# An adaLN network of two layers: the recurrent tail, attention's weights and attention as one block, with two stages re-ordered

## The reference, cut to what matters

```python
def _L0_ffn_ref(x, ...):                       # 16 steps, one for each batch of 512 tokens
    def step(c, xt):
        ft = jax.nn.sigmoid(xt @ wf.T + c @ uf.T + bf)
        it = jax.nn.sigmoid(xt @ wi.T + c @ ui.T + bi)
        gt = jnp.tanh(xt @ wc.T + c @ uc.T + bc)
        return ft * c + it * gt, None
    c_final, _ = lax.scan(step, c0, x)
    return jnp.tanh(jnp.einsum('tbi,oi->tbo', x, wo) + c_final @ uo.T + bo)

def _L1_attn_ref(x, w_qkv, w_out, head_scales, head_dirs):
    ...
    scores = jnp.where(causal, jnp.einsum('bhqd,bhkd->bhqk', q, k) * SCALE, -jnp.inf)
    scores = scores + head_scales * (q_proj[..., :, None] * k_proj[..., None, :])
    attn = jax.nn.softmax(scores, axis=-1)
    return (attn @ v, heads side by side) @ w_out

h = _layernorm(x) * (1 + ca) + sa;  x = x + ga * mixer(h)
h = _layernorm(x) * (1 + cb) + sb;  x = x + gb * _L0_ffn_ref(h)
mod = (silu(L1_c) @ L1_wmod)                   # shifts, scales and gates of layer 1
h = _layernorm(x) * (1 + ca) + sa;  x = x + ga * _L1_attn_ref(h)
h = _layernorm(x) * (1 + cb) + sb;  x = x + gb * experts(h)
```

## Time and profile before

| what | us |
| --- | --- |
| median of 3 runs | 2698.3 (2697.41 to 2700.79) |
| the profiled execution, its own time | 2689.7 |
| its span | 2687.9 |
| PE, DVE, ACT, POOL busy | 2297.5, 1619.2, 1319.7, 483.9 |
| mixer | 0 to 672 |
| recurrent part | 687 to 1036 |
| tail, `attention_weights`, attention's prologue | 1036 to 1083.6, to 1099.5, to 1162.2 |
| attention's batches | 1162.2 to 2171, some 63 each |
| router and experts | to 2688 |

### The profile page before, as it was taken

One profiled execution on the slowest core, in us unless ns is written; L12 is line 12 of the kernel. 1 busy time (PEld: TensorE's weight loads), 2 busy tenths in 40 slices (PEclk: granted clock), 3 DMA queues, 4 the chain that ended last, 5 costly groups with the idle time before them and its releaser, 6 DMA issues. The chain is left out here.

```text
span 2687.9 us, 45298 instructions
## 1 busy us (share of the span) xinstructions
PE 2297.5 (85%) x15010; PEld 1685.1 (63%) x15010; DVE 1619.2 (60%) x3537; ACT 1319.7 (49%) x2260; POOL 483.9 (18%) x397
## 2 busy tenths in 40 slices
PE   7999999999699997378888888888888875169997
PEld 6666666666588886245555555555555565158996
DVE  4667766765454443456666666666666655766664
ACT  3555565555455556235555555555555543034442
POOL 0011011100011116100000011111000022036664
PEclk8999999999799997679999999999999987579998
DMA  4200000000100000222322232233322228245542
GB/s 112 87 0 0 0 0 0 0 0 0 32 0 0 0 0 24 67 70 74 78 73 72 71 80 72 72 75 78 81 73 71 49 87 279 52 127 124 127 93 32
DMA packets 122975, 156.64 MB, mean 58 GB/s; under 512 B 26896, under 2 KB 104096, under 8 KB 122784
## 3 DMA queue, kind: packets, MB, share of 16 engines
q1 hardware_dynamic: 108576, 130.38, 17.7%
q0 software_dynamic: 14336, 25.44, 4.8%
HBM read 96.26 MB, written 58.98 MB: 58 GB/s over the span
## 5 line engine op out<-in xcount | busy, mean ns | idle before, releaser
L1483 DVE TENSOR_REDUCE at_top<-psum 128x1 f32<-128x512 f32 (+3 forms) x1024 | 446.7, 483 | 302.4 <-PE psum L1259 301.8
L1610 ACT ACTIVATE at_probs<-psum 128x512 f32<-128x512 f32 (+1 forms) x768 | 365.8, 530 | 347.8 <-PE psum L1277 345.5
L1257 PE MATMUL psum<-at_k_stack,at_q_stack 96*128 96x512 bf16 (+3 forms) x1024 | 296.1, 316 | 127.4 <-DMA at_k_stack<-qk_parts 71.9
L1275 PE MATMUL psum<-at_q_stack,at_k_stack 98*128 98x512 bf16 (+3 forms) x1024 | 289.9, 310 | 23.5 <-ACT at_probs L1610 16.8
L1257 PEld LDWEIGHTS psum<-at_k_stack,at_q_stack 96*128 96x128 bf16 x1024 | 103.3, 101 | 228.4 <-DVE at_top L1483 101.7
L1259 PE MATMUL psum<-at_mask_q,at_ident_b 128*128 128x128 bf16 x1024 | 206.9, 228 | 0.0
L1277 PE MATMUL psum<-at_mask_k,at_ident_b 128*128 128x128 bf16 x1024 | 202.9, 224 | 0.0
L1275 PEld LDWEIGHTS psum<-at_q_stack,at_k_stack 98*128 98x128 bf16 x1024 | 102.8, 100 | 116.3 <-issue 44.7
L1293 PE MATMUL psum<-at_probs,at_values 128*32 128x512 f32 (+3 forms) x2048 | 151.1, 436 | 0.9 <-ACT at_probs L1610 0.9
L2334 POOL DMA_INDIRECT out<-ex_result,slot_tokens x64 | 119.6, 1869 | 103.8 <-DVE ex_result L2466 89.2
L2512 ACT ACTIVATE ex_mid<-psum,ex_b_up 128x512 f32<-128x512 f32 x96 | 66.2, 690 | 106.2 <-PE psum L61 104.1
(11 more groups left out here) (401 smaller groups left out, 5896.5 us busy)
## 6 DMA issues: line engine op xcount, KB each, us to landing
qk_parts<-at_q_parts SPq DMA_DIRECT2D x96, 128.0 KB
qk_parts<-at_k_parts SPq DMA_DIRECT2D x96, 128.0 KB
at_q_stack<-qk_parts SPq DMA_DIRECT2D x64, 192.0 KB
at_k_stack<-qk_parts SPq DMA_DIRECT2D x64, 192.0 KB
x_residual<-in_x SPq DMA_DIRECT2D x16, 512.0 KB, 3.8
at_q_stack<-qk_parts SPq DMA_DIRECT2D x64, 128.0 KB
at_k_stack<-qk_parts SPq DMA_DIRECT2D x64, 128.0 KB
token_rows<-ro_h_tok SPq DMA_DIRECT2D x16, 512.0 KB, 3.0
```

Of the source, the lines that this page charges most:

```text
L1257: pe.matmul(out, q_stack[0:STACK, h, qt * P:(qt + 1) * P], k_stack[0:STACK, h, 0:w], start=True, stop=True)
L1275: pe.matmul(bank(bk)[:, col:col + w], k_stack[0:STACK + N_SHIFT, h, kt * P:(kt + 1) * P], q_stack[0:STACK + N_SHIFT, h, kt * P:T], start=T ...
L1483: dve.tensor_reduce(top[:, h, qt:qt + 1], bank(MAX0 + n % 2)[:, col:col + w], AX.X, ALU.max).then_inc(mxr.sem, 1)
L1610: act.activation(probs[:, slot(h), 512 * f:512 * f + w], bank(f)[:, 0:w], ACT.Exp).then_inc(ex.sem, 1)
```

## The change

`out_x` and `out_c` now live until the end of attention. The three blocks of tail, `attention_weights` and attention become one. A tail's sum, tanh and gate are all written in place in `out_x` (the sum of batch 0 on DVE, the others on POOL). Attention's buffers are pieces of the same memory: `q_stack` that of batches 0 to 3, `k_stack` 4 to 7, `probs` and `oT` 8 to 14, `o_tok` 15; the staging of the weights lies in `values`, `v_tok` and `xn`. So the first load of a stack waits until eight tails are turned (`turned`), and the first scores until all 16 are added. Each engine's tails are written between the steps of the prologue.

The modulation of layer 1 moves into the last batch of the mixer. In the mixer, DVE does all four subtractions, ahead of `dve_hT_lo`. In the batches of attention, ACT issues the rows of maxima (`act_row`), SP only stores and loads, and the side work of ACT and DVE is placed behind single pieces f of a head, the q and k copies one head later; load 1 waits until the row of group 2 of the batch under way has landed.

```diff
-        recurrent_stage(nc, t, ps, mem)
-        attention_stage(nc, t, ps, mem)
+        with ExitStack() as seam:
+            out_x = seam.enter_context(nc.sbuf_tensor("out_x", [P, NB, DK, T], F32))
+            out_c = seam.enter_context(nc.sbuf_tensor("out_c", [P, DK, T], F32))
+            recurrent_stage(nc, t, ps, mem, out_x, out_c)
+            attention_stage(nc, t, ps, mem, out_x, out_c)
...
+            else:
+                pe.wait_ge(*gs(i, 4))
+                pe.wait_ge(wmod1_in, 16)
+                for j in range(12):
+                    for k in range(DK):
+                        last = pe.matmul(bank(MOD1_BANK)[:, j * NB:(j + 1) * NB], wmod1[:, k, j * P:(j + 1) * P],
+                                         mem["silu_c1"][:, k, :], start=(k == 0), stop=(k == DK - 1))
+                last.then_inc(mod1_done, 1)
...
+            dve.wait_ge(*ms(i, 1))
+            for m in range(IK):
+                dve.tensor_tensor(dev[:, m, :], y[:, m, :], mean[:, :], ALU.subtract).then_inc(fc0.sem, 1)
             if not last_batch:
                 dve_hT_lo(dve, i + 1, False)
-            dve.wait_ge(*ms(i, 1))
-            for m in range(2, IK):
-                dve.tensor_tensor(dev[:, m, :], y[:, m, :], mean[:, :], ALU.subtract).then_inc(fc0.sem, 1)
...
-            for m in range(2):
-                if m == 0:
-                    pool.wait_ge(*ms(i, 1))
-                pool.tensor_tensor(dev[:, m, :], y[:, m, :], mean[:, :], ALU.subtract).then_inc(dv.sem, 1)
...
-            for m, ready, n in ((2, fc0, 1), (0, dv, 1), (3, fc0, 2), (1, dv, 2)):
-                act.wait_ge(*ready(i, n))
+            for m in range(IK):
+                act.wait_ge(*fc0(i, m + 1))
                 act.activation(dev[:, m, :], dev[:, m, :], ACT.Square).then_inc(sq.sem, 1)
...
+        flat = out_x[:, :, :, :].rearrange("p s k t -> p (s k t)")
+        ROW_X = DK * T
+        q_stack, k_stack = (flat[:, 4 * n * ROW_X:4 * (n + 1) * ROW_X].bitcast(BF16).rearrange("p (h t) -> p h t", h=HEADS)
+                            for n in range(2))
+        at_probs, at_oT, at_o_tok = 8 * ROW_X, 8 * ROW_X + (GROUP + 1) * 1280, 15 * ROW_X
+        probs = flat[:, at_probs:at_oT].rearrange("p (s n) -> p s n", s=GROUP + 1)
+        oT = flat[:, at_oT:at_oT + T]
+        o_tok = flat[:, at_o_tok:at_o_tok + TT * D].rearrange("p (n d) -> p n d", n=TT)
...
+        delta = out_c
+        f_q, f_k, f_v, f_o = (values[:, n, :, :].rearrange("p h c -> p (h c)").rearrange("p (k n) -> p k n", k=DK)
+                              for n in range(4))
+        f_qT, form = (v_tok[:, 2 * n:2 * n + 2, :] for n in range(2))
+        dirs, sdirs, scales = xn[0:HEADS, 0, :], xn[0:HEADS, 1, :], xn[0:HEADS, 2, 0:1]
...
+        def pe_tail(pe, b):
+            pe.wait_ge(gated, b + 1)
+            if tail_before(b) >= 0:
+                pe.wait_ge(added, tail_before(b) + 1)
+            for n in range(TT):
+                for f in range(DK):
+                    last = pe.transpose(bank(tail_bank(b) + n // 2)[:, (n % 2) * D + f * P:(n % 2) * D + (f + 1) * P],
+                                        out_x[:, b, f, n * P:(n + 1) * P], ident[:, :])
+            last.then_inc(turned, 1)
...
+            pe_tail(pe, 0)
...
+            pe_tail(pe, 6)
+            pe_tail(pe, 7)
+            pe.wait_ge(w_const, 3)
+            pe_tail(pe, HALF_X)
+            pe.wait_ge(added, HALF_X)
...
             for h in range(AHEAD):
                 for f in range(3):
                     pe_max(pe, 0, h, f)
-            pe_turn_max(pe, 0, 0)
+                if h == GROUP:
+                    pe_turn_max(pe, 0, 0)
+                pe_tail(pe, HALF_X + 1 + h)
+            pe.wait_ge(added, NB)
+            pe.wait_ge(w_lo, O_W + 1)
...
+        def dve_tail_add(dve, b):
+            dve.wait_ge(turned, b + 1)
+            tiles = x[:, b * TT:(b + 1) * TT, :]
+            k = tail_bank(b)
+            dve.tensor_tensor(tiles, tiles, ps[:, k:k + 2, :].rearrange("p k (a d) -> p (k a) d", a=2), ALU.add
+                              ).then_inc(added, 1)
...
+            dve_tail_add(dve, 6)
+            dve_tail_add(dve, 7)
+            dve_w_lo(dve, O_W)
             dve.memset(k_stack[STACK:STACK + N_SHIFT, :, :], 1.0).then_inc(const.sem, 1)
+            dve.wait_ge(w_lo, len(WEIGHTS))
             dve.memset(values[:, :, :, HD:HD + 1], 1.0).then_inc(const.sem, 1)
             dve.memset(values[:, :, :, HD + 1:], 0.0).then_inc(const.sem, 1)
-            dve_hT_lo(dve, 1)
+            dve_tail_add(dve, HALF_X)
             for h in range(AHEAD):
                 dve_max(dve, 0, h)
-            dve_neg_max(dve, 0, 0, True)
+                if h == GROUP:
+                    dve_neg_max(dve, 0, 0, True)
...
+        def act_row(act, b, g):
+            act.wait_ge(*neg(b, N_SHIFT * (g + 1)))
+            for j in range(N_SHIFT):
+                act.dma_start(q_stack[STACK + j:STACK + j + 1, GROUP * g:GROUP * (g + 1), :].rearrange(
+                    "a h (q p) -> a (h q) p", p=P), neg_top[:, j, :]).then_inc(row[g].sem, 16)
...
+        def act_tail(act, b):
+            if b == 0:
+                act.wait_ge(z_dve, 1)
+            else:
+                act.wait_ge(z_pool, b)
+            act.activation(out_x[:, b, :, :], out_x[:, b, :, :], ACT.Tanh).then_inc(tanh_done, 1)
+            act.wait_ge(tanh_done, b + 1)
+            for m in range(DK):
+                last = act.activation(out_x[:, b, m, :], out_x[:, b, m, :], ACT.Copy, scale=mod0[:, GATE_B + m, b:b + 1])
...
+                for f in range(3):
+                    act_exp(act, i, h, f, first)
+                    if f == 2 and h % GROUP == 0 and not (first and h == 0):
+                        act_keep_oT(act, *((i, h // GROUP - 1) if h else (i - 1, NG - 1)))
+                    if h == 1 and not last:
+                        if f < 2:
+                            act_qk(act, i + 1, f)
+                        else:
+                            act_qk2(act, i + 1, 0)
+                    if f == 0 and h % GROUP == 2 and not (last and h + GROUP > HEADS):
+                        g = h // GROUP
+                        act_row(act, *((i, g + 1) if g + 1 < NG else (i + 1, 0)))
+                    if h == 2 and f < 2 and not last:
+                        if f == 0:
+                            act_qk2(act, i + 1, 1)
+                        act_qk(act, i + 1, 2 + f)
+                    if h == 3 and f < 2 and not last:
...
+            act_tail(act, 0)
+            act_tail(act, 1)
+            act_tail(act, 2)
+            act.wait_ge(w_fold, 5)
+            act_w_hi(act, Q_W)
+            act_tail(act, 3)
...
+            act_tail(act, 6)
+            act_tail(act, 7)
+            act_w_hi(act, O_W)
+            for b in range(HALF_X, NB - 1):
+                act_tail(act, b)
+            act_row(act, 0, 0)
+            act_tail(act, NB - 1)
...
+        def pool_tail_sum(pool, b):
+            pool.tensor_tensor(out_x[:, b, :, :], out_x[:, b, :, :], out_c[:, :, :], ALU.add).then_inc(z_pool, 1)
...
+            for b in range(1, 4):
+                pool_tail_sum(pool, b)
             pool_rstd(pool, 0)
+            for b in range(4, 7):
+                pool_tail_sum(pool, b)
+            pool_qk3(pool, 0, (0, 1))
             pool_rstd(pool, 1)
-            pool_qk3(pool, 0)
+            pool_qk3(pool, 0, (2, 3))
+            for b in range(7, NB):
+                pool_tail_sum(pool, b)
             pool_values(pool, 0)
...
+                if isinstance(b, int) and b == 0:
+                    sp.wait_ge(turned, HALF_X)
+            elif g == 1:
+                sp.wait_ge(*(loaded[0](0, loaded[0].per) if isinstance(b, int) and b == 0 else row[2](b - 1, row[2].per)))
...
-        def sp_row(sp, b, g):
-            sp.wait_ge(*neg(b, N_SHIFT * (g + 1)))
-            for j in range(N_SHIFT):
-                sp.dma_start(q_stack[STACK + j:STACK + j + 1, GROUP * g:GROUP * (g + 1), :].rearrange(
-                    "a h (q p) -> a (h q) p", p=P), neg_top[:, j, :]).then_inc(row[g].sem, 16)
...
+            for side in range(2):
+                sp_store(sp, i + 1, side)
+            for g in range(NG):
+                sp_load(sp, i + 1, g)
```

497 lines of the change are left out of this document (213 added, 284 removed).

## The result

The changed kernel takes 2681.6 us (median of 4 runs, 2679.5 to 2686.0), the one before 2697.9 on the same chip: ratio 0.9945, interval 0.9929 to 0.9961. It is faster by 16 us, 0.55%. The forecast was 2621 with a range of 2555 to 2668, so the sign was right, but the time is 60 us above the forecast and 14 above the range.

The account below looks back on a forecast made before the run. PE was taken to bound mixer and attention, gains coming only from its gaps, and hand-over chains the seam. -12 - 26 - 39 = -77 on 2689.7 gives 2612.7; with 8.6 carried from profile to median, 2621 us, range 2555 to 2668.

Parts of the forecast that it names:

- Mixer, -12: Mixer: with all four subtractions on DVE ahead of the low half, PE's variance wait goes; -12 us, bounds -8 to -13.
- Seam, -26: Recurrence's end to first scores: three blocks become one, first Exp at about 1136, before 1162; -26 us, bounds -40 to -10.
- (a): Seam: the chain from first weight DMA to batch 1's transposed input on ACT takes 41.9 us, now starting at 1036.
- (b): Seam: ACT does tails 3 to 7 within that chain, 12.3 us plus 3 for hand-overs; tail 7 turned at about 1095.
- Rival E: Seam: POOL's sums block DVE's two-input operations, some ten losing 1 to 2.4 us each; +20, 2641 us; chance 0.07.
- Attention batches, -39: Attention loop: earlier loads, less clock loss and shorter waits for maxima give -2.6 us a batch, times 15; bounds -90 to +15.
- Step (1): Attention batches: rows of maxima go from SP to ACT, so the load isn't held behind them; 0.3 to 0.4 us a group.
- Step (2): Attention batches: q and k copies one head later, between single Exps and reductions; the load goes out 1 us earlier.
- ACT's issues: Attention batches: each row DMA issue on ACT takes 0.58 us, mostly hidden; 0.3 to 0.4 us a group on the path.
- B: Attention loop gains nothing, as the load still comes late and ACT's row issues eat the splitting's gain; 2660 us; chance 0.20.
- the loss that eats the 38 us: Attention loop: a loss that just eats the 38 us of mixer and seam; chance 0.03.
- C: Attention loop: ACT stands at the row's wait with Exps behind it, 4.7 us a batch; slower, 2730 us; chance 0.09.

Follow-up runs that it names:

- mixer_only: The kernel before with the mixer's re-ordering alone (four subtractions on DVE, ahead of the low half): 2681.6 against 2693.3 us, ratio 0.9953.
- mix_c_sums: qk_early with group 2's row issued one piece earlier on ACT, other rows on POOL, and POOL's tail sums moved later in the seam: 2587.7 us, ratio 0.9627.
- qk_early: The changed kernel with the q and k copies back at their old places behind heads 0 and 1, in two lumps: 2616.2 us, ratio 0.9704.
- qk_late: The changed kernel with its old attention batches put back, except that the q and k copies stay one head later: 2659.1 us, ratio 0.9864.
- rows_sp: The changed kernel with only the rows of maxima back on SP in the old order: 2661.6 us, ratio 0.9910.
- loop_rows_act: The changed kernel with its attention batches as before, except that ACT issues the rows of maxima: 2637.8 us, ratio 0.9788.

## Why the prediction was wrong, point by point

**Bounds and stages.** Right: each stage moved by its own wait, and the sum over the span tells nothing.

**Mixer, -12.** Right by mechanism and size where it stands alone (mixer_only). In the changed kernel 10 us of it are left. PE's first matmul of the recurrent part stands at 691.6 us before, at 679.9 in mixer_only and at 681.6 in the changed kernel (680.9 to 682.1 in eight kernels built on it). Most of the 1.7 us between comes up in the mixer's last batch, into which layer 1's modulation was moved: its matmuls hold PE from 648.1 to 654.6 us, at a place where PE waits 4.6 us in mixer_only, and the batch is 1.8 us longer. The prediction put this term at nothing, "if the cover fails: some 2 us, once": the cover failed.

**Seam, -26.** Right in its sum, 27.3, and less so in its terms. Tail 7 was turned at about 1088 and not 1095 in a trace that is 10 us ahead, so (a) and (b) were 3 us longer than reckoned. The load took 11.5 us from issue to first maxima (1088.48 to 1100.0) for 12.5, and its wait was 8.8 of PE's. The seven heads took 3.1 to 4.1 us each, 25 in all with the scores' start, for 27. **Rival E's mechanism was there** although the total was not its: next to POOL's sums the four norms of each of two batches took 7.4 and 6.3 us and not 1.4, two low halves 5.0 and not 1.3. The rule of the Trainium skill that the prediction named ("SBUF — State Buffer", section "SBUF: two separate sides") agrees with the low halves, which have two inputs in SBUF. The norms have one large input, and what the prediction took from the rule, operations with two SBUF inputs, did not name them. That same rule of the Trainium skill also names VectorE operations in a two-port mode; whether the norms ran in one no run here shows. mix_c_sums puts the price of these rows on the seam's end at 8.6 us, so that the sum came out right in spite of them is partly luck: other terms must have been too long by about as much.

**Attention batches, -39.** Wrong; measured +29.4, or +2.0 us a batch (65.9 for 63.9; the prediction's 63.3 for before was 0.6 low) where -2.6 was forecast. Three steps failed.

- *The order on SP.* Step (1) of this part read the earlier trace rows as a load that is held up behind the row, and asked only when the load would be released and what would queue behind ACT's wait. It did not ask what the load does to the row. One queue had kept the small, urgent DMAs ahead of the load's 0.8 MB in packets of 4 KB. With the row on a second queue, and the load released a moment earlier, the row's packets share the DMA engines with the load's, and it lands in 7.1 us in place of 1.7. Head 8 waits, and the half clock comes with it: heads 7 and 8 +5.3 us, which is what heads 9 and 10 saved. The prediction's list of signs did name a new wait for the row, but put it down to ACT.
- *The late copies.* Step (2) had the load's time nearly right: it was issued at 28.1 us of a batch, before at 28.5, so 0.4 us earlier where 1 was forecast. It counted that as a gain of the same size. In truth the row, issued at 29.6 us and before at 27.1, came just behind it. With the copies at their old places (qk_early) the load goes out at 23.6, the row at 29.7, and a batch takes 61.5 us, 2.4 under before, and 2616 us in all. That this is near the 2.6 and the 2621 that were forecast is luck, as the terms are others: heads 9 and 10 give 5.1, and heads 0, 2, 3, 7 and 8 take 3.1 of it back. That the lateness costs anything on a single queue is not shown (qk_late).
- *ACT's issues.* Priced at 0.3 to 0.4 us for each of four groups, 1.4 us a batch, and then left out of the sum. Changed against rows_sp they cost 1.5 us. So the price was right and the addition wrong. The 1.7 us at heads 2 and 3 that the late copies were to take, and that "comes out of the wait for the load", were 0.2 (qk_late, rows_sp); most of the 1.4 measured there is ACT's row, and it came on top, since the load wait had been replaced and not shortened.

The 0.9 us for the split of DVE's lumps at heads 11 and 13 is not there either: heads 11 to 13 take 9.9 us for 10.2, and heads 4 to 6 lose 0.2. The +0.6 for heads 14 and 15 was -0.2. What the split is worth shows only where the load does not limit: 2.3 us at heads 7 and 8, qk_early against loop_rows_act.

**Rivals.** The time lies between two of them, 22 us above B (no gain in the loop, 2660) and 16 under the loss that eats the 38 us. C had the loop's sign but the wrong place: PE's wait for Exps rose by 4 us only. A loop that loses without C's mechanism had 0.03, and the range, to 2668, left it out. The bound of +1 a batch was too tight by the prediction's own ends: a load 3 us late in place of 1 early turns -2.6 into +1.4, without any price for ACT's issues. None of these ends is the new wait.

**The carry-over** of 8.6 us from profile to median did not hold for the changed kernel, whose profiled execution was 1.7 us above its median. This error of 10 us went the prediction's way: by the profiled executions the forecast was 2612.7 and 2683.3 came, so the stages were wrong by 71 us, and the carry-over hid 10 of them.

## What to carry to other kernels

When a DMA moves to another engine's queue, look at what stood behind it in the old one: the order there may have protected it, and a small transfer that is issued behind a large one waits with it; here even 4 to 7 us behind were not enough for it to land as fast as ahead of it. Before calling a delay harmless because nothing waits for the delayed thing, look at what it will then coincide with. When one wait is removed, the next ones in line (here side work in lumps on ACT and DVE) are worth splitting only afterwards.
